# Squares of every second tile on GpSimd, another order on VectorE, shorter layer norms and null keys in a decoder block

## The chip, the cores and the metric

The kernel runs on one core of a Trainium2 chip. The metric is the device time of one launch in microseconds: 911.29 us, the median of three runs of the kernel before (907.23 to 911.75). Everything is float32; the large projections are made in three passes of a reduced type that together keep float32's accuracy.

The core has five engines with a queue each, and what stands in a queue is done in order: TensorE (PE; matmuls and transposes, results in PSUM), VectorE (DVE), ScalarE (ACT), GpSimd (POOL; it reaches SBUF alone, not PSUM) and SyncE (SP; here it issues all DMAs). They wait for one another by semaphores.

## The reference

16 batch elements of 256 tokens of 128 features go through one decoder block with a layer norm behind each of its three parts:

```
x = layernorm(x + attn(x));  x = layernorm(x + xattn(x, ctx));  x = layernorm(x + ffn(x))

attn:  xn = (x - mu) * rsqrt(var + 1e-5) * gamma
       q, k, v = xn @ w_q, xn @ w_kv            # 16 heads of 64
       k, v = [null_k, k], [null_v, v]          # 2 null keys and values per head
       q, k = l2norm(q) * q_scale, l2norm(k) * k_scale
       sim = 8 * q k^T - slope_h * distance;  causal mask;  softmax;  @ v;  @ w_out
xattn: 16 heads of 8 over 64 context tokens
ffn:   y = (x W1^T + b1) W2^T + b2              # no nonlinearity; one of 8 weight sets per 2 elements
```

The L2 norms need the sum of the squares of each head of q and k: per batch element 256 tokens (two tiles of 128) times 2048 values. The squares, their sums, a floor of 1e-24 and an inverse square root are separate steps.

## The kernel before

The work is written as one queue per engine, with an `iteration(i)` in each. There are 16 iterations. Iteration i does the attention of element i, the cross attention of element i-1, the end of the cross attention and the feed-forward of element i-2, and, ahead of time, the projections of q and k of element i+2 and of the values of element i+1, and the transposes of q and k of element i+1. The order inside each queue is written out by hand; there is no planner. A tile is 128 tokens; t is 0 or 1.

What the change touches, engine by engine:

- Layer norms (`ln_begin`, `newton`, `ln_end` on VectorE, `ln_seed` on ScalarE). VectorE makes mean and variance (L869, L872) and adds epsilon in an operation of its own (L875). ScalarE makes a first inverse square root by a logarithm and an exponential (`rsqrt_seed`, L1270 and L1272). VectorE refines it by one Newton step (three operations: L879, L881, L883) and normalises the tiles (L892). There are four norms: ln1 on the input, ln2 behind the attention, ln3 behind the cross attention, ln4 behind the feed-forward. The norms of q and k use the same seed and Newton step (`qk_seed`, `norms`).
- Squares of q and k. ScalarE copies the projections out of PSUM (`copy_qk`, L1308, eight chunks per element, four per tile) and squares them (`square_qk`, L1316, one operation per tile and half, 128x1024 each). VectorE sums them per head (`sum_squares`, L986) and applies the floor (`floor_squares`, L992). All go through one buffer `sq`. GpSimd scales q and k by the norms (`norm_qk`, L1569). For tile 1 the squares stand at the very end of ScalarE's iteration, two iterations ahead, in front of `copy_nullraw` (L1325), which empties the bank psJ0 that `project_v(i+1, 0)` of the next iteration (L443 to L445) takes.
- Masks. TensorE makes scores into three banks psS (`scores`, L555); VectorE adds the position bias and takes the row minimum (`mask_scores`, L1030, one operation per head); a bank is free again when its chunk is masked. Tile 0 has four chunks of four heads, tile 1 eight of two. ScalarE exponentiates head by head (L1350) and in between copies values (`copy_v`, L1330) and other results out of PSUM. VectorE makes the denominators (L1043 to L1047), GpSimd scales the probabilities (`norm_probs`, L1578), TensorE turns them (`turn_probs`, L577), and so on.
- Layer norm 3 in an iteration: `add_y2` (L1102) and `ln3_begin` come first on VectorE, `ln3_end` between the second and third chunk of tile 0. TensorE turns the result (`x2_turn`, L696) behind the first pair of scores of tile 1, ScalarE copies it (L1405), and the feed-forward (L704) uses it.
- GpSimd begins an iteration with `x1_plus_bias` (L1611), which waits for `add_y2`, then `x2_plus_bias` (L1618), which waits for `ln3_end`, then `norm_probs`.
- The start. The null keys are normalised, turned, and multiplied by the query weights of their head: 16 matmuls over 64 rows each, into two banks (`merged_nulls`, L460; each is two instructions). VectorE splits the product into two parts (`split_wn`). The null values are multiplied by the output weights (`null_values`, L468) right behind, into the bank psT0, and copied out by VectorE (`copy_null_v`). Both stand in TensorE's queue before the second half of the q and k projections of element 1.

Of the kernel before, what the change touches and what calls it, by code (L numbers as in the profile page):

```python
# [113 lines left out]
def program(nc, x, ctxT, gamma, w_q, w_kv, wqT, wvT, wout, nk, nvT, q_scale, k_scale,  # L114
            xwq, xwk, xwv, xbq, xbk, xbv, xwoT, xbo, w1b, w2T, b2, ident_in, dist_in, nullbias_in,
            hmask_in, hmask2_in, out):
    with ExitStack() as ctx:  # L117
# [99 lines left out]
        ln_small = sb("ln_small", [P, 5 * len(LN), NT])  # L217
        ve, lv, sd, nw, rs = ({n: ln_small[:, len(LN) * q + k, :] for k, n in enumerate(LN)} for q in range(5))
# [5 lines left out]
        nvT_s = pr[0][:, 8:10, :].rearrange("p h k -> p (h k)").rearrange("p (c n) -> p c n", c=HP)  # L224
# [51 lines left out]
        nkssq_ready = sem("nkssq_ready")  # L276
        nkrow_ready = sem("nkrow_ready")
# [52 lines left out]
        qk_normed = sem("qk_normed")  # L330
        probs_normed = sem("probs_normed")
# [99 lines left out]
        def _(pe):  # L431
# [16 lines left out]
            def turn_null_keys():  # L448

                pe.wait_ge(nkrow_ready, 1)  # L450
                take('T0', nkT_copied, 1)
# [268 lines left out]
            null_values()  # L720
# [12 lines left out]
            def iteration(i, w, g):  # L733
# [22 lines left out]
                if a:  # L756
                    project_v(i + 1, 3)
                turn_probs(i, 0)
# [96 lines left out]
        def _(dve):  # L855
# [10 lines left out]
            def ln_begin(name, src, tiles, count):  # L866
# [18 lines left out]
            def ln_end(name, src, dst, tiles, count):  # L885

                dve.wait_ge(seed_ready[name], count)
                a, z = tiles[0], tiles[-1] + 1
                steps.mark(newton(sd[name][:, a:z], ve[name][:, a:z], nw[name][:, a:z], rs[name][:, a:z], 0.5))
# [29 lines left out]

            def null_squares():  # L920
# [19 lines left out]
            def split_wn():  # L940
                dve.wait_ge(wn_ready, 1)
                hi, lo = (w[:].rearrange("p (c r n) -> p c r n", r=2, n=NULLS) for w in (wn_hi, wn_lo))
                ps = [psT[r][:, 0:NN // 2].rearrange("p (c n) -> p c n", n=NULLS) for r in range(2)]
                for r in range(2):
                    steps.mark(dve.tensor_copy(hi[:, :, r, :], ps[r]))
                steps.wait(dve)
                for r in range(2):
                    last = dve.tensor_tensor(lo[:, :, r, :], ps[r], hi[:, :, r, :].bitcast(F32), ALU.subtract)
                    if r == 0:
                        steps.mark(last)  # L950
                last.then_inc(wn_split, 1)
# [32 lines left out]
            def sum_squares(n, t, half):  # L984
                dve.wait_ge(qk_squared, 2 * (NT * n + t) + half + 1)
# [138 lines left out]

            ln1_begin(0)
# [6 lines left out]
            ln1_begin(1)  # L1132
            null_squares()
# [15 lines left out]
            copy_null_v()  # L1149
# [17 lines left out]
            def iteration(i, w, g):  # L1167
# [96 lines left out]
        def _(act):  # L1264
# [9 lines left out]
            def ln_seed(name, tiles, count):  # L1274
                act.wait_ge(var_ready[name], count)
                a, z = tiles[0], tiles[-1] + 1
                rsqrt_seed(ve[name][:, a:z], lv[name][:, a:z], sd[name][:, a:z], 1.0).then_inc(seed_ready[name], 1)
# [11 lines left out]
            def copy_nkT():  # L1289
                act.wait_ge(nkT_ready, 1)  # L1290
                act.activation(nkT[:], psT[0][:, 0:NN], ACT.Copy).then_inc(nkT_copied, 1)
# [18 lines left out]
            def square_qk(n, t, half):  # L1310
                act.wait_ge(qk_copied_act, chunks_to(QK_ACT, n, 4 * t + 2 * half + 1))
                act.wait_ge(qk_copied_dve, chunks_to(QK_DVE, n, 4 * t + 2 * half + 1))
                if half == 0:
                    need(act, ssq_ready, NT * n + t)
# [409 lines left out]
```

## Time and profile before

| | |
|---|---|
| runs | 907.23, 911.29, 911.75 us |
| profiled execution | 912.71 us, its span 910.9 us |
| TensorE (PE) | 801.6 us busy, 88% |
| VectorE (DVE) | 719.1 us, 79% |
| ScalarE (ACT) | 662.7 us, 73% |
| GpSimd (POOL) | 424.3 us, 47% |

The span runs from the first to the last instruction of the profiled execution. Busy is the time in which an engine worked; the shares are averages over a start of some 54 us, 16 iterations of 51 to 53 us and an end of some 40 us. A line such as L1316 is a line of the kernel; PEld is the loading of weights into TensorE, which overlaps with its matmuls.

### The profile page before, as it was taken

Reading aid. Unit: us, or ns where it says so; the run is one execution under the profiler, and the core shown is the slowest. Engines: PE = TensorE matmul, PEld = TensorE weight load, DVE = VectorE, ACT = ScalarE, POOL = GpSimd, SP = SyncE. Lnnn points to the kernel's source line nnn. Section 1 sums busy time; section 2 is a strip of 40 time slices with the busy share of each in tenths; the row PEclk is TensorE's granted clock in tenths of the full one; section 3 lists DMA queues with packets and bytes.
Section 4 is the critical chain, followed back from the end, with each engine's and each line's share of the span. In section 5 each row is a group of like instructions: output and inputs, shape, how many; then the busy total and the mean of one; then the engine's idle time right before and its main releaser. Section 6 shows DMA issues by size and latency. Waiting matters only on the chain. (4 is left out here: it accounts for less than half of the span.)

```text
span 910.9 us, 19543 instructions
## 1 busy us (share of the span) xinstructions
PE 801.6 (88%) x6469; PEld 581.0 (64%) x6469; DVE 719.1 (79%) x2504; ACT 662.7 (73%) x1994; POOL 424.3 (47%) x356
## 2 busy tenths in 40 slices
PE   5879989898998989898998989899998989887953
PEld 3657657575776757576675757576675757665632
DVE  6584677898969897898969897888969887887744
ACT  4386686968777786968778796978778696867522
POOL 0317164472727355371736446271736547173611
PEclk9599999999999999999999999999999999999965
DMA  6000001000100001000100000000010001000000
GB/s 211 6 7 1 13 2 36 2 7 13 31 13 8 13 8 36 2 6 13 31 13 8 13 7 24 13 7 14 10 34 7 8 1 31 7 6 8 7 1 12
DMA packets 26418, 15.62 MB, mean 17 GB/s; under 512 B 4304, under 2 KB 25552, under 8 KB 26320
## 3 DMA queue, kind: packets, MB, share of 16 engines
q1 hardware_dynamic: 26320, 14.38, 5.5%
q8 instruction: 53, 0.87, 0.4%
q14 instruction: 45, 0.37, 0.1%
HBM read 12.27 MB, written 2.10 MB: 16 GB/s over the span
## 5 line engine op out<-in xcount | busy, mean ns | idle before, releaser
L1578 POOL TENSOR_TENSOR pr<-pr,rden 128x512 f32<-128x512 f32 x192 | 192.9, 1040 | 170.3 <-DVE rden L1045 170.3
L1350 ACT ACTIVATE pr<-pr,nmin 128x256 f32<-128x256 f32 (+1 forms) x512 | 225.3, 446 | 0.0
L1030 DVE CUSTOM_DVE_ANT_0 pr<-psS,alibi,nullmin 128x256 f32<-128x256 f32 (+1 forms) x512 | 180.3, 412 | 17.0 <-PE psS L555 16.9
L577 PE MATMUL psT<-ident,pr 128*128 128x128 f32 x768 | 124.6, 287 | 19.9 <-POOL pr L1578 19.7
L555 PE MATMUL psS<-kT,qT 64*128 64x256 f32 (+1 forms) x1024 | 110.6, 344 | 32.1 <-DVE nmin L1030 30.4
L1569 POOL TENSOR_TENSOR qk<-qk,rn 128x1024 f32<-128x1024 f32 x64 | 121.0, 1911 | 32.9 <-DVE rn L883 32.9
L577 PEld LDWEIGHTS psT<-ident,pr 128*128 128x128 f32 x768 | 80.9, 141 | 57.9 <-POOL pr L1578 28.6
L555 PEld LDWEIGHTS psS<-kT,qT 64*128 64x128 f32 x1024 | 78.3, 187 | 58.6 <-issue 56.6
L1308 ACT ACTIVATE qk<-psJ 128x512 f32<-128x512 f32 x128 | 75.5, 591 | 40.3 <-PE psJ L445 40.1
L1350 ACT ACTIVATION_READ_ACCUMULATOR pr<-pr,nmin 128x1 f32 x512 | 98.7, 193 | 0.0
L986 DVE TENSOR_REDUCE ssq<-sq 128x16 f32<-128x1024 f32 x64 | 77.6, 1212 | 22.8 <-ACT sq L1316 22.8
L1380 ACT ACTIVATE xp<-xp 128x1024 f32<-128x1024 f32 x32 | 33.8, 1058 | 73.1 <-DVE xp L1090 73.1
L1611 POOL TENSOR_TENSOR x1b<-x,bo 128x256 f32<-128x256 f32 x16 | 11.7, 732 | 159.8 <-DVE r L1102 147.2
L600 PE MATMUL psY<-pT,val 128*64 128x128 f32 x1024 | 82.0, 286 | 4.2 <-ACT aoT L1336 2.5
L1585 POOL TENSOR_TENSOR xp<-xp,xrden 128x1024 f32<-128x1024 f32 x32 | 60.9, 1903 | 42.0 <-DVE xrden L1097 42.0
L600 PEld LDWEIGHTS psY<-pT,val 128*64 128x64 f32 x1024 | 53.5, 136 | 37.7 <-issue 26.7
L537 PE MATMUL psS<-ident,qk 128*128 128x128 f32 x512 | 69.8, 276 | 3.5 <-DVE qT L1020 2.9
L1367 ACT ACTIVATE pT<-psT 128x512 f32<-128x512 f32 x112 | 65.5, 585 | 6.5 <-PE psT L577 6.5
L443 PE MATMUL psJ<-wqk_hi,xnT_hi 128*128 128x512 f32 x128 | 63.9, 499 | 5.2 <-DVE xnT_lo L980 2.9
L1316 ACT ACTIVATE sq<-qk 128x1024 f32<-128x1024 f32 x64 | 65.8, 1052 | 0.4
L537 PEld LDWEIGHTS psS<-ident,qk 128*128 128x128 f32 x512 | 56.7, 140 | 9.4 <-DVE qT L1020 4.0
L1270 ACT ACTIVATE ln_small<-ln_small 128x2 f32<-128x2 f32 x64 | 12.7, 199 | 68.3 <-DVE ln_small L875 68.2
(147 smaller groups left out, 1692.7 us busy)
## 6 DMA issues: line engine op xcount, KB each, us to landing
w1s<-w1b SPq DMA_DIRECT2D x8, 258.0 KB, 3.0
xres<-x SPq DMA_DIRECT2D x16, 128.0 KB, 2.1
w2s<-w2T SPq DMA_DIRECT2D x8, 256.0 KB, 3.2
out<-x SPq DMA_DIRECT2D x16, 128.0 KB, 1.8
xin<-x SPq DMA_DIRECT2D x15, 128.0 KB, 2.4
pr<-w_kv SPq DMA_DIRECT2D x2, 512.0 KB, 5.8
pr<-w_q SPq DMA_DIRECT2D x1, 512.0 KB, 3.6
wo<-wout SPq DMA_DIRECT2D x1, 512.0 KB, 6.4
```

What stands on the lines that cost most here:

```text
L537: mm = pe.transpose(psS[isk][:, P * j:P * (j + 1)], qk[n % 2][t][:, col:col + P], ident[:])
L555: mm = pe.matmul(psS[score_bank(t, c)][:, keys * j:keys * (j + 1)], qT[r, h // 2, P * t:P * (t + 1)], kT[r, h // 2, 0:keys], start=True, s ...
L577: mm = pe.transpose(psT[c % 2][:, P * j:P * (j + 1)], pr[t][:, h, P * kt:P * (kt + 1)], ident[:])
L600: mm = pe.matmul(bank[r, P * pair:P * (pair + 1)], val[b % 2][:, kt, DH * h:DH * (h + 1)], pT[c % 4][:, P * j:P * (j + 1)], start=(kt == 0 ...
L986: steps.mark(dve.tensor_reduce(ssq[:, t, H * half:H * (half + 1)], sq[:, HD * half:HD * (half + 1)].rearrange("p (h d) -> p h d", d=DH), A ...
L1030: dve.tensor_tensor_reduce(pr[t][:, h, :], psS[score_bank(t, c)][:, keys * j:keys * (j + 1)], alibi[:, h, SEQ - keys:SEQ], 1.0, nullmin[:, ...
L1308: act.activation(qk[n % 2][t][:, 512 * j:512 * (j + 1)], psJ[c % 2][:], ACT.Copy).then_inc(qk_copied_act, 1)
L1316: act.activation(sq[:, col], qk[n % 2][t][:, col], ACT.Square).then_inc(qk_squared, 1)
L1350: act.activation(pr[t][:, h, :], pr[t][:, h, :], ACT.Exp, bias=nmin[:, t, h:h + 1], scale=-1.0, accum_out=dparts[:, t, h, 0:1]).then_inc(e ...
L1367: act.activation(pT[c % 4][:], psT[c % 2][:], ACT.Copy).then_inc(pT_copied_act, 1)
L1569: pool.tensor_tensor(v, v, rn[:, t, H * k:H * (k + 1)].unsqueeze(2).broadcast_to([P, H, DH]), ALU.mult).then_inc(qk_normed, 1)
L1578: pool.tensor_tensor(pr[t][:, hs, :], pr[t][:, hs, :], rden[:, t, hs].unsqueeze(2).broadcast_to([P, heads, P * (t + 1)]), ALU.mult).then_i ...
```

## The change

- ScalarE squares tile 0 alone. GpSimd squares tile 1 with a multiplication, for element 0 at the start and for element i+1 at the beginning of iteration i, behind `x1_plus_bias`; from iteration 2 on it first waits for the variances of layer norm 3. The new semaphore `qk_squared_pool` tells VectorE.
- On VectorE, all four chunks of tile 0 are masked and shifted before `ln3_end`; the first sum of squares of tile 1 comes behind the second chunk of tile 1, the second behind the third; the floor behind all masks of the iteration. `copy_pT(i, 0)` comes before `add_h2`. ScalarE's `qk_seed(i+1, 1)` comes behind its exponentials.
- Epsilon is no longer added by VectorE: ScalarE's logarithm takes it as a bias (from a small tile `eps`), and the Newton step adds it in its second operation. `ln_seed` waits for both variances and for `eps`.
- The null keys are laid out in a cleared tile so that one matmul over 128 rows makes two heads: 8 matmuls into one bank. The copy that lays them out becomes two. `split_wn` has two operations instead of four.
- `null_values` moves into iteration 0, ahead of its first `turn_probs`, and `copy_null_v` behind the fourth chunk of tile 1 there. Its input moves to another part of SBUF.

```diff
             def ln_begin(name, src, tiles, count):
                 for t in tiles:
-                    steps.mark(dve.bn_aggr(mv[name][:, t, :], st[name][:, t, :]))
-                steps.wait(dve)
-                a, z = tiles[0], tiles[-1] + 1
-                dve.tensor_scalar(ve[name][:, a:z], mv[name][:, a:z, 1], EPS, None, ALU.add).then_inc(var_ready[name], 1)
+                    dve.bn_aggr(mv[name][:, t, :], st[name][:, t, :]).then_inc(var_ready[name], 1)
...
-            def newton(y0, v, tmp, res, half):
-                steps.mark(dve.tensor_tensor(tmp, y0, y0, ALU.mult))
+            def newton(y0, v, tmp, res, half, floor=None):
+                steps.mark(dve.scalar_tensor_tensor(out=tmp, in0=y0, scalar=-half, in1=y0, op0=ALU.mult, op1=ALU.mult))
                 steps.wait(dve)
-                steps.mark(dve.scalar_tensor_tensor(out=tmp, in0=tmp, scalar=-half, in1=v, op0=ALU.mult, op1=ALU.mult))
+                if floor is None:
+                    steps.mark(dve.tensor_tensor(tmp, v, tmp, ALU.mult))
+                else:
+                    steps.mark(dve.scalar_tensor_tensor(out=tmp, in0=v, scalar=floor, in1=tmp, op0=ALU.add, op1=ALU.mult))
...
             def merged_nulls():
                 pe.wait_ge(h_loaded, 16 * 2)
                 take('T0', wn_split, 1)
-                take('T1', wn_split, 1)
-                for h in list(range(0, H, 2)) + list(range(1, H, 2)):
-                    r = slice(DH * (h % 2), DH * (h % 2) + DH)
-                    mm = pe.matmul(psT[h % 2][:, NULLS * (h // 2):NULLS * (h // 2 + 1)], wqT_s[r, h // 2, :],
-                                   nkT[r, NULLS * h:NULLS * (h + 1)], start=True, stop=True)
+                for c in range(HP):
+                    pair = slice(2 * NULLS * c, 2 * NULLS * (c + 1))
+                    mm = pe.matmul(psT[0][:, pair], wqT_s[:, c, :], nkT[:, pair], start=True, stop=True)
                 mm.then_inc(wn_ready, 1)
...
             merged_nulls()
-            null_values()
             project_nulls(0)
...
                 if a:
                     project_v(i + 1, 3)
+                if i == 0:
+                    null_values()
                 turn_probs(i, 0)
...
# VectorE's iteration
-                mask_scores(i, 0, (0, 1))
+                mask_scores(i, 0, (0, 1, 2, 3))
+                null_shift(i, 0)
                 if e:
                     ln3_end(i - 2)
-                mask_scores(i, 0, (2, 3))
-                null_shift(i, 0)
-                if p:
-                    sum_squares(i + 1, 1, 0)
                 need(dve, probsT_ready, PC * i)
                 for k in range(8):
                     mask_scores(i, 1, (k,))
                     if k == 1:
                         if p:
-                            sum_squares(i + 1, 1, 1)
-                            floor_squares(1)
+                            sum_squares(i + 1, 1, 0)
                         denominators(i, 0)
+                    if k == 2 and p:
+                        sum_squares(i + 1, 1, 1)
                     if k == 3:
+                        if i == 0:
+                            copy_null_v()
+                        copy_pT(i, 0)
                         if e:
                             add_h2(i - 2)
-                        copy_pT(i, 0)
                     if k == 5:
                         copy_pT(i, 2)
                 null_shift(i, 1)
+                if p:
+                    floor_squares(1)
...
# ScalarE
-            def rsqrt_seed(v, tmp, res, scale):
-                steps.mark(act.activation(tmp, v, ACT.Ln, scale=scale))
+            def rsqrt_seed(v, tmp, res, scale, floor=0.0):
+                steps.mark(act.activation(tmp, v, ACT.Ln, bias=floor, scale=scale))
...
                 if a:
                     copy_v(i + 1, 3)
-                if p:
-                    qk_seed(i + 1, 1)
                 copy_pnT(i, 0)
...
                 copy_aoT(i, 0, 1)
+                if p:
+                    qk_seed(i + 1, 1)
...
                     copy_qk(i + 2, 7)
-                    square_qk(i + 2, 1, 0)
-                    square_qk(i + 2, 1, 1)
                     copy_nullraw(i + 2)
...
# GpSimd
+            def square_qk(n, half):
+                pool.wait_ge(qk_copied_act, chunks_to(QK_ACT, n, 4 + 2 * half + 1))
+                if half == 0:
+                    pool.wait_ge(ssq_ready, NT * n + 1)
+                v = qk[n % 2][1][:, HD * half:HD * (half + 1)]
+                pool.tensor_tensor(sq[:, HD * half:HD * (half + 1)], v, v, ALU.mult).then_inc(qk_squared_pool, 1)
...
+            square_qk(0, 0)
+            square_qk(0, 1)
             norm_qk(0, 0)
             norm_qk(0, 1)
...
                 if c:
                     x1_plus_bias(i - 1)
+                if p:
+                    if e:
+                        pool.wait_ge(var_ready["ln3"], NT * (i - 1))
+                    square_qk(i + 1, 0)
+                    square_qk(i + 1, 1)
                 if e:
                     x2_plus_bias(i - 2, (i - 2) // 2)
                 norm_probs(i, 0)
```

## Rows read from the trace of the kernel before

**Rows 1.** Page, 40 slices of the span: TensorE's granted clock in tenths.

```profile
PEclk9599999999999999999999999999999999999965
```

**Rows 2.** Waits, whole span: who <- whom, us in total, times, longest.

```profile
PE psS L555 <- DVE nmin L1030: 30.4, 32, 1.5
```

**Rows 3.** Timeline, TensorE, iteration 7: start, us, instruction, [idle before <- releaser].

```profile
420.26 0.44 PE L627 MATMUL psT<-ident,x 128*128 128x128 f32 x2
420.75 0.50 PE L443 MATMUL psJ<-wv_hi,xnT_hi 128*128 128x512 f32 x1
...
425.09 1.14 PE L555 MATMUL psS<-kT,qT 64*128 64x256 f32 x8 [0.78 <-DVE nmin L1030]
426.16 0.44 PE L696 MATMUL psT<-ident,x 128*128 128x128 f32 x2
426.35 0.49 PE L443 MATMUL psJ<-wv_hi,xnT_hi 128*128 128x512 f32 x1
...
431.98 0.66 PE L577 MATMUL psT<-ident,pr 128*128 128x128 f32 x4 [1.17 <-POOL pr L1578]
...
434.77 0.27 PE L616 MATMUL psJ<-ident,pnn 128*32 128x128 f32 x1 [0.48 <-ACT val L1330]
```

**Rows 4.** Timeline, ScalarE, the same iteration.

```profile
418.59 1.99 ACT L1316 ACTIVATE sq<-qk 128x1024 f32<-128x1024 f32 x2
...
421.75 0.60 ACT L1330 ACTIVATE val<-psJ 128x512 f32<-128x512 f32 x1 [0.45 <-PE psJ L445]
422.25 0.39 ACT L1350 ACTIVATE pr<-pr,nmin 128x128 f32<-128x128 f32 x1
...
427.70 0.37 ACT L1405 ACTIVATE x1T<-psT 128x256 f32<-128x256 f32 x1
...
429.50 0.23 ACT L1355 ACTIVATE dparts<-nulld 128x32 f32<-128x32 f32 x1
...
434.03 0.59 ACT L1330 ACTIVATE val<-psJ 128x512 f32<-128x512 f32 x1
```

**Rows 5.** Timeline, TensorE, iteration 1.

```profile
109.13 0.44 PE L627 MATMUL psT<-ident,x 128*128 128x128 f32 x2
109.95 0.50 PE L443 MATMUL psJ<-wv_hi,xnT_hi 128*128 128x512 f32 x1 [0.38 <-ACT nullraw L1325]
...
123.71 0.27 PE L616 MATMUL psJ<-ident,pnn 128*32 128x128 f32 x1 [0.97 <-ACT val L1330]
```

**Rows 6.** Page, groups of instructions: count | busy us, mean ns | idle before, releaser.

```profile
L986 DVE TENSOR_REDUCE ssq<-sq 128x16 f32<-128x1024 f32 x64 | 77.6, 1212 | 22.8 <-ACT sq L1316 22.8
...
L1585 POOL TENSOR_TENSOR xp<-xp,xrden 128x1024 f32<-128x1024 f32 x32 | 60.9, 1903 | 42.0 <-DVE xrden L1097 42.0
```

**Rows 7.** Timeline, GpSimd, iteration 7.

```profile
419.27 0.73 POOL L1611 TENSOR_TENSOR x1b<-x,bo 128x256 f32<-128x256 f32 x1 [9.29 <-DVE r L1102]
```

**Rows 8.** Timeline, VectorE, iteration 7.

```profile
420.50 0.35 DVE L1030 CUSTOM_DVE_ANT_0 pr<-psS,alibi,nullmin 128x128 f32<-128x128 f32 x1 [0.30 <-PE psS L555]
...
422.68 0.16 DVE L879 TENSOR_TENSOR ln_small<-ln_small 128x2 f32<-128x2 f32 x1
...
423.78 0.34 DVE L1030 CUSTOM_DVE_ANT_0 pr<-psS,alibi,nullmin 128x128 f32<-128x128 f32 x1
...
430.26 0.20 DVE L1043 TENSOR_REDUCE den<-dparts 128x16 f32<-128x48 f32 x1
...
430.90 0.48 DVE L1030 CUSTOM_DVE_ANT_0 pr<-psS,alibi,nullmin 128x256 f32<-128x256 f32 x1
```

**Rows 9.** Chain that ended last, near the span's end: start, us, what.

```profile
901.11 0.18 DVE ln_small L875
```

**Rows 10.** Timeline, TensorE, the start.

```profile
28.88 6.16 PE L460 MATMUL psT<-nkT,pr 64*128 64x2 f32 x32
...
35.77 3.59 PE L468 MATMUL psT<-wo,pr 128*32 128x128 f32 x16 [0.73 <-DVE wn_lo L948]
```

**Rows 11.** One line, L958 on VectorE: ns min/median/max, first and last start.

```profile
L958 DVE TENSOR_TENSOR wv_lo<-pr,wv_hi x2: 693/1483/2273, 25.6 to 29.9; 128x512 fp32r<-128x512 f32 x2
```

More of the change, by code:

```diff
@@ L216, in program @@
         mv = {n: sb(f"{n}_mv", [P, NT, 2]) for n in LN}
-        ln_small = sb("ln_small", [P, 5 * len(LN), NT])
-        ve, lv, sd, nw, rs = ({n: ln_small[:, len(LN) * q + k, :] for k, n in enumerate(LN)} for q in range(5))
+        eps = sb("eps", [P, 1])
+        ln_small = sb("ln_small", [P, 4 * len(LN), NT])
+        lv, sd, nw, rs = ({n: ln_small[:, len(LN) * q + k, :] for k, n in enumerate(LN)} for q in range(4))
         wqk_raw = pr[1][:, 0:8, :].rearrange("p h k -> p (h k)")
@@ L223, in program @@
         wqT_s = pr[0][:, 0:8, :]
-        nvT_s = pr[0][:, 8:10, :].rearrange("p h k -> p (h k)").rearrange("p (c n) -> p c n", c=HP)
+        nvT_s = xp[1][:, 8:12, :].rearrange("p h k -> p (h k)").rearrange("p (c n) -> p c n", c=HP)
         dist = x3[:].rearrange("p t d -> p (t d)")
@@ L276, in program @@
         nkssq_ready = sem("nkssq_ready")
+        eps_ready = sem("eps_ready")
+        nkT_cleared = sem("nkT_cleared")
         nkrow_ready = sem("nkrow_ready")
@@ L330, in program @@
         qk_normed = sem("qk_normed")
+        qk_squared_pool = sem("qk_squared_pool")
         probs_normed = sem("probs_normed")
@@ L450, in turn_null_keys @@
                 pe.wait_ge(nkrow_ready, 1)
-                take('T0', nkT_copied, 1)
+                take('T0', nkT_copied, 2)
                 pe.transpose(psT[0][:, 0:NN], nkrow, ident[0:NN, 0:NN]).then_inc(nkT_ready, 1)
@@ L887, in ln_end @@
                 dve.wait_ge(seed_ready[name], count)
+                dve.wait_ge(var_ready[name], NT * count)
                 a, z = tiles[0], tiles[-1] + 1
-                steps.mark(newton(sd[name][:, a:z], ve[name][:, a:z], nw[name][:, a:z], rs[name][:, a:z], 0.5))
+                steps.mark(newton(sd[name][:, a:z], mv[name][:, a:z, 1], nw[name][:, a:z], rs[name][:, a:z], 0.5, EPS))
                 steps.wait(dve)
@@ L918, in split_wqk, with clear_nkT @@
                                   ALU.subtract).then_inc(wsplit_ready, 1)
+            def clear_nkT():
+                dve.memset(nkT[:], 0.0).then_inc(nkT_cleared, 1)
             def null_squares():
@@ L941, in split_wn @@
                 dve.wait_ge(wn_ready, 1)
[L942 to L945, printed above, removed]
+                steps.mark(dve.tensor_copy(wn_hi[:], psT[0][:, 0:NN]))
                 steps.wait(dve)
[L947 to L951, printed above, removed]
+                dve.tensor_tensor(wn_lo[:], psT[0][:, 0:NN], wn_hi[:].bitcast(F32), ALU.subtract).then_inc(wn_split, 1)
             def split_wv(c):
@@ L984, in sum_squares @@
             def sum_squares(n, t, half):
-                dve.wait_ge(qk_squared, 2 * (NT * n + t) + half + 1)
+                dve.wait_ge(qk_squared if t == 0 else qk_squared_pool, 2 * n + half + 1)
                 steps.mark(dve.tensor_reduce(ssq[:, t, H * half:H * (half + 1)],
@@ L1122, in ln4_end @@
                 ln_end("ln4", r3, x3, (0, 1), b + 1).then_inc(x3_ready, 1)
+            dve.memset(eps[:], EPS).then_inc(eps_ready, 1)
             ln1_begin(0)
@@ L1132, in _ @@
             ln1_begin(1)
+            clear_nkT()
             null_squares()
@@ L1274, in ln_seed @@
             def ln_seed(name, tiles, count):
-                act.wait_ge(var_ready[name], count)
+                act.wait_ge(eps_ready, 1)
+                act.wait_ge(var_ready[name], NT * count)
                 a, z = tiles[0], tiles[-1] + 1
-                rsqrt_seed(ve[name][:, a:z], lv[name][:, a:z], sd[name][:, a:z], 1.0).then_inc(seed_ready[name], 1)
+                rsqrt_seed(mv[name][:, a:z, 1], lv[name][:, a:z], sd[name][:, a:z], 1.0, eps[:]).then_inc(seed_ready[name], 1)
             def null_keys_seed():
@@ L1290, in copy_nkT @@
                 act.wait_ge(nkT_ready, 1)
-                act.activation(nkT[:], psT[0][:, 0:NN], ACT.Copy).then_inc(nkT_copied, 1)
+                act.wait_ge(nkT_cleared, 1)
+                for r in range(2):
+                    rows = slice(DH * r, DH * (r + 1))
+                    act.activation(nkT[rows, :].rearrange("p (c r n) -> p c r n", r=2, n=NULLS)[:, :, r, :],
+                                   psT[0][rows, 0:NN].rearrange("p (c r n) -> p c r n", r=2, n=NULLS)[:, :, r, :],
+                                   ACT.Copy).then_inc(nkT_copied, 1)
             def context_kv():
@@ L1308, in copy_qk @@
                 act.activation(qk[n % 2][t][:, 512 * j:512 * (j + 1)], psJ[c % 2][:], ACT.Copy).then_inc(qk_copied_act, 1)
-            def square_qk(n, t, half):
-                act.wait_ge(qk_copied_act, chunks_to(QK_ACT, n, 4 * t + 2 * half + 1))
-                act.wait_ge(qk_copied_dve, chunks_to(QK_DVE, n, 4 * t + 2 * half + 1))
+            def square_qk(n, half):
+                act.wait_ge(qk_copied_act, chunks_to(QK_ACT, n, 2 * half + 1))
                 if half == 0:
-                    need(act, ssq_ready, NT * n + t)
+                    need(act, ssq_ready, NT * n)
                 col = slice(HD * half, HD * (half + 1))
-                act.activation(sq[:, col], qk[n % 2][t][:, col], ACT.Square).then_inc(qk_squared, 1)
+                act.activation(sq[:, col], qk[n % 2][0][:, col], ACT.Square).then_inc(qk_squared, 1)
             def qk_seed(n, t):
@@ L1431, in _ @@
             copy_qk(1, 5)
-            square_qk(1, 0, 0)
+            square_qk(1, 0)
             copy_qk(1, 6)
             copy_qk(1, 7)
-            square_qk(1, 0, 1)
+            square_qk(1, 1)
             copy_v(0, 0)
@@ L1506, in iteration @@
                     copy_qk(i + 2, 2)
-                    square_qk(i + 2, 0, 0)
+                    square_qk(i + 2, 0)
                 copy_aoT(i, 1, 0)
@@ L1515, in iteration @@
                     copy_qk(i + 2, 3)
-                    square_qk(i + 2, 0, 1)
+                    square_qk(i + 2, 1)
                 copy_pT(i, 11)
@@ L1619, in x2_plus_bias @@
                                    ALU.add).then_inc(x2b_ready, 1)
+            square_qk(0, 0)
+            square_qk(0, 1)
             norm_qk(0, 0)
```

8 lines of the change are left out of this document (1 added, 7 removed).

## The prediction

> **What bounds the kernel now.** I read four views in this order: the busy shares and the clock of the page, the waits of the whole span, the timeline of one iteration engine by engine, and the first and last stretches. The clock row [rows 1] shows full clock from the start's end to the epilogue, so between them a microsecond of TensorE work has one price. TensorE is 88% busy. The waits [rows 2] name what stops it most: the masks on VectorE, twice in each of 16 iterations, 30.4 us in all.
>
> The timeline of iteration 7, which starts at 419.2 and repeats from iteration 2 to 14 within 0.03 us, puts this in place. Behind 438.8 TensorE shows no idle time until the next iteration's first scores. All its idle time lies in a front of about 20 us: 0.78 us and once more about a microsecond for masks, 1.17 us for the probabilities that GpSimd scales, 0.48 us for a value copy on ScalarE [rows 3]. So only what shortens the front shortens an iteration, and the last gate in it counts. That gate is the row at 434.77: the turn of the null probabilities waits for `copy_v(i+1, 3)`, which starts on ScalarE at 434.03 [rows 4]. From the first exponential at 422.25 to that copy ScalarE shows no idle time: 16 exponentials of tile 0, three copies, the null exponentials at 429.50, eight exponentials of tile 1, another copy. It is a solid chain of 11.8 us, and its start is set by `copy_v(i+1, 0)` at 421.75, which had waited for `project_v(i+1, 0)` on TensorE.
>
> Iteration 1 is a natural test. It has no end of layer norm 3 among its masks, so VectorE is ahead there; yet TensorE only waits longer for the same copy, 0.97 us in place of 0.48 [rows 5]. What VectorE gives in the front is not passed on; what ScalarE gives is.
>
> **The change, part by part.**
>
> *Squares of tile 1.* Two of the four squares per batch element leave ScalarE: 1.99 us at the end of an iteration, 418.59 to 420.58 [rows 4]. Behind them stands the copy of the raw null scores, and only that frees the bank of `project_v(i+1, 0)`. TensorE starts the turn of x1 at 420.26 and the projection at 420.75, 0.49 us later; the same pair of a turn and a projection, ungated, takes 426.35 - 426.16 = 0.19 us [rows 3]. Without the squares the null scores are copied about a microsecond earlier, so the projection comes 0.30 us earlier, and with it the chain, the null exponentials (429.20), the value copy (433.73) and the turn of the nulls. The rest of the 1.99 us becomes idle time of ScalarE in front of `copy_v`. In iteration 1 the distance is 109.95 - 109.13 = 0.82 us [rows 5], which gives 0.63.
>
> *The same squares on GpSimd.* The trace has no square there. The nearest row is a two-input operation of the same size, 1.90 us [rows 6]; from below, ScalarE's 1.0 us for one; from above, twice the row, since both operands are full streams here and one is a broadcast there. I take 1.90. GpSimd is free after `x1_plus_bias`, at 419.27 + 0.73 = 420.00 [rows 7], and has nothing due until layer norm 3 ends, so the squares run from 420.0 to 423.8, beside the masks, and nothing waits for them until the third chunk of tile 1.
>
> The Trainium skill (GPSIMD Engine Reference, section 3.1, Elementwise) puts a two-input operation at about 2.6 cycles an element. For 1024 elements that is an estimate of 2.2 us, where the rows here have 1.90; the squares would end at 424.4, and the sum stays.
>
> *Order on VectorE.* The first eight masks take 422.68 - 420.50 = 2.18 us, the end of layer norm 3 after them 423.78 - 422.68 = 1.10 us [rows 8]. Now all 16 masks come first (to 424.9), the null shift, then the end of layer norm 3 from 425.07 to 426.2. The third chunk is masked 1.1 us earlier, and the 0.78 us wait at 425.09 goes. But the next thing in TensorE's queue is the turn of x2, which starts at 426.16 now and at about 426.3 then: one wait takes the other's place. Behind it the second pair of scores of tile 1 comes about 0.9 us earlier, since the first sum of squares (1.21 us [rows 6]) no longer stands before the first chunk. The denominators find VectorE free as soon as the null exponentials end, and start at 429.5 where they now start at 430.26; turning the probabilities starts at 431.2 in place of 431.98 [rows 3, 8]. TensorE then reaches the turn of the nulls at 433.4 and waits there a microsecond, for a copy that is 0.30 us earlier and no more. The second sum of squares now stands before the third head group: from 429.5, 0.64 us for the denominators (430.26 to 430.90 [rows 8]), 0.8 for a chunk, 1.2 for the sum and 0.5 for the first mask end at 432.6, and ScalarE wants it at 432.75. That margin is thin. The floor and the square-root seed of tile 1 move behind the masks and into idle time of ScalarE before the cross exponentials: nothing.
>
> *No constant step in layer norms.* One operation of 0.17 us and its hand-over, 0.20 us, leaves each of four norms per iteration; in the body all lie beside TensorE work. At the end three follow each other with nothing beside them (the norm of the last iteration's attention and the last two, as at 901.11 [rows 9]): 0.6 us, less a second wait per seed on ScalarE, which no row shows (0 to 0.05 us). I take 0.5 there, and 0.03 per iteration off the gain above, where the seed of layer norm 4 stands in the chain.
>
> *The start.* The product of the null keys shrinks from 32 to 16 instructions (6.16 us, about 3 saved), the null values leave (3.59 us) [rows 10]. The first saving is not collected: VectorE is late in its place. A split of the value weights that met a GpSimd operation took 2.27 us and 0.69 without [rows 11]; now the squares of element 0 run at 24 us, meet the Newton steps, and push the same splits back, so the split null keys come about 0.2 us later than now. The second saving is collected, but at 46 us the squares of element 1 meet the end of layer norm 1 on VectorE, a whole GpSimd operation (1.9), and in iteration 0 the null values share a bank with the turn of the probabilities, which waits until VectorE copies them out behind three chunks and a sum of squares: about 0.8 more. 3.6 - 0.2 - 1.9 - 0.8 = 0.7 us gained. Ends: 3.5 gained (no meeting) and 2 lost (iteration 0 alone).
>
> The Trainium skill (SBUF — State Buffer, Who interferes with whom) says VectorE and GpSimd lock one pair of ports for a whole instruction, and that a VectorE operation with one SBUF input outside a two-port mode is free of it. The 2.27 us above agree. Were there no lock, the start would gain 3 us and the sum be about 7.7; by the rule, 5.3.
>
> **Sum.** 13 iterations of 0.27 are 3.5, iteration 1 gives 0.6, the start 0.7, the end 0.5: 5.3 us. The profiled execution took 912.71 us (span 910.9, 1.8 around it), 1.4 over the median of 911.29; 5.3 less is 907.4 for it and 906.0 for a median.
>
> **Rivals.**
>
> *Nothing arrives.* The projection's 0.3 us may not be there (ends of matmuls are modelled), or the thin margin at the third head group eats it: a mask 0.3 us late stops ScalarE, and the chain ends where it ends now. For it: the margin of 0.15 us. Against: iteration 1, where a later projection went with a later chain. What is left is start and end, 0 to 3 us: 909.5.
>
> *The front pays in full.* If the turn of the nulls isn't the last gate, the 0.8 us at turning the probabilities are kept: 13 x 0.8 + 1.2 = 11.6, so 899.7. Against it stands iteration 1 [rows 5].
>
> *Slower: the squares outlast the masks.* The null shift and the end of layer norm 3 start at 425.0, with both inputs in SBUF, the kind that waits for GpSimd. From 420.0 that allows 2.5 us a square; from there each excess delays x2. ScalarE takes the copy of x2 at 427.70 [rows 4], now 427.4, in the middle of its chain, with 0.65 us in hand. At twice the row (3.8 us) the squares end at 427.6, x2 is turned by 429.25, ScalarE stops for 1.85 us, less 0.3 gained: 13 x 1.55 = 20, so 931. For it: no row has two full streams on GpSimd. Against: every row of 1024 elements, with other broadcasts, is 1.9.
>
> **How the numbers follow.** Forecast 0.52 (903 to 909.5), nothing arrives 0.21, full front 0.12, slower 0.15. A run of this kernel tells about 0.5%, 4.6 us, from no change. The forecast, 5.3 with 2 on either side, is over that in six of ten: 0.33; with the full front, 0.45 or a little more. Same: the rest of the forecast and nothing arrives, 0.40. Slower: 0.14. The range runs from the full front to a slower case of small excess, 899.5 to 914.
>
> **What would show it.** Right: the projection 0.2 us behind the turn of x1 in every iteration; a wait of the turn of x2 for layer norm 3 that is new, about 0.9 us; the wait for the third chunk gone; the wait of the turn of the nulls grown to a microsecond; an iteration 0.27 us shorter; squares of 1.9 us on GpSimd ending before the null shift. Wrong: squares over 2.5 us, an idle gap of ScalarE inside its chain, or iterations shortened by 0.5 us or more, which would mean that I have the wrong gate.

## The result and the profile after

The changed kernel takes 912.62 us, the median of 20 runs from 910.76 to 913.64; the kernel before 909.22, the median of 20 from 907.23 to 913.15. The ratio is 1.003, with a 95% interval of 1.0017 to 1.0043: a loss of about 3 us where a gain of 5.3 was forecast. The profiled execution of the changed kernel took 911.29 us (span 909.5).

The medians can only be read with TensorE's granted clock: the later runs of the kernel before, which list it, lie mostly in two groups, 907.3 to 910.3 us with a mean granted clock of 0.972 and 911.4 to 913.5 with 0.966 (a few with 0.968 lie at 910.3 to 912.2), the profile ahead of the prediction (912.71 us, 0.966) is of the second, and the changed kernel's 20 runs all lie between 0.959 and 0.963.

The body did what was forecast. TensorE's first scores of iterations 7 and 8 start at 419.46 and 471.7, and the two lengths that alternate from iteration 2 on are 50.80 and 52.22 us where they were 51.07 and 52.49 (one or two early ones are 0.2 to 0.4 longer in both): 0.27 less each. First the waits of TensorE in the whole span of the changed kernel: who waited for whom, us in total, times, longest; then its timeline in iteration 7.

```profile
PE psT L698 <- DVE x L896: 19.9, 15, 3.3
PE psT L579 <- POOL pr L1589: 17.1, 16, 2.3
PE psJ L618 <- ACT val L1339: 13.8, 14, 1.1
PE psS L557 <- DVE nmin L1030: 9.1, 19, 1.1
```

```profile
420.55 0.44 PE L629 MATMUL psT<-ident,x 128*128 128x128 f32 x2
420.74 0.48 PE L447 MATMUL psJ<-wv_hi,xnT_hi 128*128 128x512 f32 x1
...
422.11 1.16 PE L557 MATMUL psS<-kT,qT 64*128 64x128 f32 x16 [0.42 <-DVE nmin L1030]
...
424.70 1.13 PE L557 MATMUL psS<-kT,qT 64*128 64x256 f32 x8
427.02 0.44 PE L698 MATMUL psT<-ident,x 128*128 128x128 f32 x2 [1.18 <-DVE x L896]
...
431.46 0.66 PE L579 MATMUL psT<-ident,pr 128*128 128x128 f32 x4 [0.90 <-POOL pr L1589]
...
434.74 0.27 PE L618 MATMUL psJ<-ident,pnn 128*32 128x128 f32 x1 [0.97 <-ACT val L1339]
```

Against [rows 2, 3] the reader sees each mark that the prediction asked for. The projection stands 0.19 us behind the turn of x1 (it was 0.49), the 0.78 us wait for the masks of the third chunk, ahead of tile 1's first scores, is gone, the turn of x2 has a new one of 1.18 (0.9 forecast), and the turn of the null probabilities waits 0.97. One wait was not forecast: at 422.11 TensorE stands 0.42 us before the second pair of chunks of tile 0, since the masks that free their banks stand at the same distance behind the first scores as before (2.65 us) and do not come earlier with the projection. The masks' waits fell from 30.4 us to 9.1, but 19.9 came at the turn of x2 in their place.

So the loss lies ahead of iteration 2, whose first scores start at 162.2 where they started at 160.6. The first scores of iterations 0 and 2, of the kernel before and then of the changed one:

```profile
54.71 1.16 PE L555 MATMUL psS<-kT,qT 64*128 64x128 f32 x16 [0.29 <-ACT kT L1341]
...
160.59 1.16 PE L555 MATMUL psS<-kT,qT 64*128 64x128 f32 x16
```

```profile
52.58 1.77 PE L557 MATMUL psS<-kT,qT 64*128 64x128 f32 x16 [0.29 <-ACT kT L1350]
...
162.17 1.16 PE L557 MATMUL psS<-kT,qT 64*128 64x128 f32 x16
```

The next rows are GpSimd, VectorE and TensorE of the changed kernel at the end of iteration 0, where nothing in the prediction looked.

```profile
104.28 0.73 POOL L1622 TENSOR_TENSOR x1b<-x,bo 128x256 f32<-128x256 f32 x1 [12.60 <-DVE x L896]
104.97 3.78 POOL L1581 TENSOR_TENSOR sq<-qk 128x1024 f32<-128x1024 f32 x2
```

```profile
104.45 0.61 DVE L879 SCALAR_TENSOR_TENSOR newt<-seedq 128x32 f32<-128x32 f32 x1 [0.25 <-ACT seedq L1275]
105.09 1.82 DVE L882 TENSOR_TENSOR newt<-ssq,newt 128x32 f32<-128x32 f32 x1
106.94 1.85 DVE L886 SCALAR_TENSOR_TENSOR rn<-newt,seedq 128x32 f32<-128x32 f32 x1
108.72 0.68 DVE L1020 COPY qT<-psS 128x512 f32<-128x512 f32 x1
```

```profile
109.65 1.16 PE L557 MATMUL psS<-kT,qT 64*128 64x128 f32 x16 [2.68 <-DVE qT L1020]
```

The squares of element 2 start as soon as `x1_plus_bias` ends. VectorE is then in `norms(2, 0)`: two of its operations, which take 0.19 us each when no GpSimd operation runs beside them, take 1.82 and 1.85 and end with GpSimd's. The last copy of qT is queued behind them, and TensorE waits 2.68 us for it. From iteration 2 on GpSimd first waits for the statistics of layer norm 3, so this pair doesn't meet. The same Newton step of the other tile does meet a GpSimd operation (L1605) in the body, 0.97 us at 450.01 in iteration 7, but there TensorE has other work and shows no wait.

The Trainium skill (SBUF — State Buffer, Who interferes with whom) says that a VectorE instruction with both inputs in SBUF contends with a GpSimd instruction that reads SBUF, that the one issued first keeps the ports for its whole length, and that a reduction never contends. The trace agrees: the held operations end with a GpSimd instruction, and a sum of squares beside GpSimd's scaling, at 30.33, took its 1.21 us.

The waits have a second price. Stretches of the changed kernel, in columns us, TensorE's busy time, granted clock, DMA share and GB/s:

```profile
48.60:50.60 2.00, 0.00 (x1) 1.00 0.00 0
53.00:56.40 3.40, 3.40 (x21) 0.51 0.01 2
106.90:109.60 2.70, 0.07 (x1) 1.00 0.01 3
111.00:114.40 3.40, 3.40 (x21) 0.50 0.00 0
```

Twice TensorE stood idle at full clock and then worked at half clock, 1.2 GHz, a few microseconds later; that the idle time brings the half clock is not shown by these rows, but the first experiment takes one of the two waits away, and its stretch goes with it. The stretch at 53.0 lies on the first scores of iteration 0, the one at 111.0 on the front of iteration 1. The idle time ahead of the first is the meeting that was priced (GpSimd's squares of element 1 hold L884), and between the two stands the bank of the null values:

```profile
47.35 1.77 DVE L884 SCALAR_TENSOR_TENSOR ln_small<-ln_mv,ln_small 128x2 f32<-128x2 f32 x1
...
66.74 0.27 DVE L963 COPY null_v<-psT 32x128 f32<-32x128 f32 x1
```

```profile
50.62 1.09 PE L539 MATMUL psS<-ident,qk 128*128 128x128 f32 x8 [2.01 <-DVE qT L1020]
...
62.96 1.94 PE L470 MATMUL psT<-wo,xp 128*32 128x128 f32 x16
67.16 0.63 PE L579 MATMUL psT<-ident,pr 128*128 128x128 f32 x4 [2.27 <-POOL pr L1589]
```

The last row names GpSimd, but it had scaled the first chunk by 65.0 (63.98 and a microsecond); what ends at 67.0 is the copy of the null values out of the same bank.

### The profile page after: what moved, and what is told of

The parts are those of the page before. It is cut to its first block and busy times, and to the rows that moved or that the text cites. A ratio compares the mean times of both kernels' runs of the same rounds, so it can differ in the third digit from the quotient of the medians.

```text
span 909.5 us, 19500 instructions
## 1 busy us (share of the span) xinstructions
PE 795.4 (87%) x6453; PEld 579.0 (64%) x6453; DVE 716.8 (79%) x2440; ACT 644.2 (71%) x1963; POOL 484.5 (53%) x388
## 5 line engine op out<-in xcount | busy, mean ns | idle before, releaser
L1581 POOL TENSOR_TENSOR sq<-qk 128x1024 f32<-128x1024 f32 x32 | 60.0, 1895 | 30.0 <-DVE ssq L992 29.1
L1273 ACT ACTIVATE ln_small<-ln_mv,eps 128x2 f32<-128x2 f32 x64 | 18.7, 292 | 65.4 <-DVE ln_mv L875 65.4
```

## The experiments

All times are medians, beside runs of the kernel before on the same chip; ratios are to that kernel, with 95% intervals. Periods are from first scores to first scores.

### Hold the squares of element 2

```
                 if p:
+                    if i >= 1:
+                        pool.wait_ge(rn_ready, NT * (i + 1) + 1)
                     if e:
```

> From iteration 1 on, GpSimd's squares of batch element i+1 wait until VectorE has normalised element i+1's first tile (in the changed kernel they met that Newton step once, at 104.97 us). Theory (the squares hold VectorE, VectorE holds the last copy of qT, and TensorE waits 2.68 us at 109.65 and falls to half clock behind it): iteration 0 is shorter by 2.7 us (57.07 to 54.4), iteration 1 by 0.6 more where the half-clock stretch at 111 is gone, all others stay: about 3.3 us less than the changed kernel, 909.3. Rival (the Newton step isn't what is late; the wait moves to another gate): the wait at the first scores of iteration 1 stays above 2 us, time within 0.7 us of the changed kernel.

909.74 us, ratio 0.9993 (0.9974 to 1.0012). Iteration 0 took 54.64 us and iteration 1 51.87. GpSimd, then TensorE:

```profile
106.36 3.75 POOL L1581 TENSOR_TENSOR sq<-qk 128x1024 f32<-128x1024 f32 x2 [0.58 <-DVE rn L886]
```

```profile
107.67 1.16 PE L557 MATMUL psS<-kT,qT 64*128 64x128 f32 x16
```

And the Newton step on VectorE that had taken 1.82:

```profile
105.86 0.19 DVE L882 TENSOR_TENSOR newt<-ssq,newt 128x32 f32<-128x32 f32 x1
```

The wait and the half-clock stretch behind it are gone: iteration 0 is 2.43 us shorter, iteration 1 0.65, and the median is 2.9 lower. The theory holds. The wait of 2.01 us ahead of iteration 0's first scores is still there, and the half-clock stretch behind it is 6.9 us long in this profile (50.6 to 57.5) where it was 3.4.

### The null values on the other bank

```
-                take('T0', nullv_copied, 1)
+                take('T1', nullv_copied, 1)
-                    mm = pe.matmul(psT[0][0:NN, 0:P], ...
+                    mm = pe.matmul(psT[1][0:NN, 0:P], ...
-                dve.tensor_copy(null_v[:], psT[0][0:NN, 0:P]) ...
+                dve.tensor_copy(null_v[:], psT[1][0:NN, 0:P]) ...
```

> The null values keep their new place in iteration 0 but go to the other of the two turning banks. Theory (the first turn of the probabilities waits for VectorE's copy of the null values, though the page names GpSimd, which had scaled the first chunk at about 65.0): the turn starts at about 65.2 in place of 67.16, iteration 0 is 1.9 us shorter and the time is 910.7. Rival (GpSimd's scaling, as the page names it): the wait of 2.27 us stays and the time is within 0.5 us of the changed kernel.

911.47 us, ratio 1.0008 (0.9989 to 1.0027); iteration 0 took 56.33. TensorE:

```profile
65.16 0.66 PE L579 MATMUL psT<-ident,pr 128*128 128x128 f32 x4 [0.37 <-POOL pr L1589]
...
67.25 0.63 PE L579 MATMUL psT<-ident,pr 128*128 128x128 f32 x4 [0.37 <-DVE null_v L963]
```

The turn starts where it was expected, so the releaser on the page was the wrong one. Of its 2 us only 0.74 reach the end of iteration 0, where 1.9 was expected: the second turn now waits for that copy, and the null turn behind it for a value copy.

### Epsilon on VectorE again

```
+                dve.tensor_scalar(ve[name][:, a:z], mv[name][:, a:z, 1], EPS, None, ALU.add).then_inc(var_ready[name], NT)
...
-                rsqrt_seed(mv[name][:, a:z, 1], lv[name][:, a:z], sd[name][:, a:z], 1.0, eps[:])
+                rsqrt_seed(ve[name][:, a:z], lv[name][:, a:z], sd[name][:, a:z], 1.0)
```

> Layer norms alone as before: VectorE adds epsilon with an operation of its own, ScalarE's logarithm has no column for its bias; all else as in the changed kernel. Theory (the logarithm with a column takes 0.29 us in place of 0.20 and eats half of the 0.17 us operation): the last two norms take 0.05 us longer each, iterations stay within 0.05 us, the time within 0.5 us of the changed kernel. Rival 1 (my prediction, 0.2 us per norm at the end): 0.6 us slower. Rival 2 (the column costs more than it saves, over the whole body): 1 us or more faster.

933.69 us, ratio 1.0259 (1.0230 to 1.0289), most periods 52.01 and 53.42. None of the three expectations is near. GpSimd, VectorE and TensorE in iteration 7:

```profile
443.88 3.76 POOL L1575 TENSOR_TENSOR qk<-qk,rn 128x1024 f32<-128x1024 f32 x2
```

```profile
444.65 1.16 DVE L878 TENSOR_SCALAR ln_small<-ln_mv 128x2 f32<-128x2 f32 x1
445.72 0.47 DVE L1033 CUSTOM_DVE_ANT_0 pr<-psS,alibi,nullmin 128x256 f32<-128x256 f32 x1
```

```profile
446.75 1.13 PE L557 MATMUL psS<-kT,qT 64*128 64x256 f32 x8 [1.04 <-DVE nmin L1033]
```

An addition of 0.17 us, met by GpSimd's first scaling (443.88 to 445.8), takes 1.16; the masks queued behind it are late, and TensorE waits 1.04 us for them. This operation has one input in SBUF; the same section of the Trainium skill lists its kind among those that can take both port pairs, and so wait for GpSimd, and the row agrees.

### Epsilon on VectorE in layer norms 1 to 3

```
+                if name != "ln4":
+                    dve.tensor_scalar(ve[name][:, a:z], mv[name][:, a:z, 1], EPS, None, ALU.add) ...
```

> VectorE adds epsilon with an operation of its own in layer norms 1, 2 and 3, and not in layer norm 4; all else as in the changed kernel. With all four norms so, an iteration took 1.21 us more (52.01 for 50.80) and the time was 933.7. Theory (only the operation of layer norm 4 matters: in the new order of VectorE it starts at 444.65 while GpSimd scales queries, is held for 1.16 us, and the masks of the last chunk behind it are late): periods go back to 50.8 and 52.2 within 0.1 us, time within 1 us of 912.6. Rival (the operations of the other norms delay the chain of ScalarE too): periods stay over 51.5, time over 922.

917.77 us, ratio 1.0079 (1.0052 to 1.0105), periods 50.97 and 52.40. Of the 1.21 us, 1.04 go with layer norm 4 alone, as the theory had it; the other three cost 0.18 more per iteration and not under 0.1, and the time missed the expected 912.6 by 5 us. In its profile the start is longer too (iterations 0 and 1 are 57.61 and 53.79): its two half-clock stretches there are twice as long as in the changed kernel's (51.7 to 58.6 and 109.8 to 116.6), and there is one more at 840.2 to 847.0. Why they are longer was not followed.

### All squares on ScalarE, the rest as changed

```
+                    square_second(i + 2, 0)
+                    square_second(i + 2, 1)
                     copy_nullraw(i + 2)
```

The added function is ScalarE's square of the second tile; it is also called for elements 0 and 1 in the start (not shown), and the calls in GpSimd's part go.

> All squares on ScalarE as before; the order on VectorE, the layer norms and the null keys and values as in the changed kernel. Theory (the 0.27 us per iteration come from ScalarE's freed end alone, VectorE's order is not passed on): periods of iterations 2 to 14 return to 51.07 and 52.49 within 0.06 us; no operation of VectorE is held in the start, so the waits of TensorE at 50.62 (2.01 us) and 109.65 (2.68 us) go and the first scores start 1.5 to 2 us earlier than 52.6. Sum against the changed kernel: 3.5 + 0.6 more, 2.7 + 1.7 + 1.2 less: 911.3. Rival (VectorE's order gives the 0.27 us): periods stay at 50.80 and 52.22, time 907.5.

911.71 us, ratio 1.0015 (0.9996 to 1.0034), most periods 51.12 and 52.53: without the squares' move the rest of the change gives the body nothing (before: 51.07 and 52.49). First scores of iteration 0:

```profile
48.57 1.16 PE L557 MATMUL psS<-kT,qT 64*128 64x128 f32 x16 [0.29 <-ACT kT L1357]
```

One Newton step of the start, in the changed kernel and here:

```profile
25.73 1.82 DVE L882 TENSOR_TENSOR newt<-ssq,newt 128x32 f32<-128x32 f32 x1
```

```profile
24.50 0.19 DVE L882 TENSOR_TENSOR newt<-ssq,newt 128x32 f32<-128x32 f32 x1
```

The first scores are 4.0 us earlier than in the changed kernel, where 1.5 to 2 was expected. Two meetings make it up: in the changed kernel the squares of element 0 hold the Newton steps at 24 us, and the null projections start at 34.90 where they start at 32.51 here (2.4), and the wait at 50.62 is 2.01 us long where 0.40 are left here (1.6). The wait of 2.68 us ahead of iteration 1 is gone.

### The kernel before with the squares alone

```
+                if c and p:
+                    pool.wait_ge(rn_ready, NT * (i + 1) + 1)
+                    if e:
+                        pool.wait_ge(var_ready["ln3"], i - 1)
+                    square_qk(i + 1, 0)
+                    square_qk(i + 1, 1)
```

ScalarE's two squares at the end of the iteration go (not shown).

> The kernel before with one part of the change: the second tile's squares of elements 2 and up on GpSimd, behind VectorE's normalisation of the first tile and behind the statistics of layer norm 3; VectorE's order, epsilon, null keys and values as before. Theory (the 0.27 us come from ScalarE's freed end, but only the new order takes the end of layer norm 3 out of the squares' way): the end of layer norm 3 at 422.7 in iteration 7 is held until the squares end at about 423.8, the masks behind it come a microsecond later, and periods grow to 51.3 to 52.1 in place of 51.07, time 913 to 923. Rival (the squares alone give the gain): periods 50.80 and 52.22, time 906.

922.76 us, ratio 1.0130 (1.0104 to 1.0155), periods 52.19 and 53.60, a little over the expected range. VectorE, then TensorE in iteration 7, then a stretch of iteration 8:

```profile
423.66 1.42 DVE L880 TENSOR_TENSOR ln_small<-ln_small 128x2 f32<-128x2 f32 x1
```

```profile
427.34 1.13 PE L556 MATMUL psS<-kT,qT 64*128 64x256 f32 x8 [2.05 <-DVE nmin L1031]
```

```profile
481.70:484.90 3.20, 3.20 (x13) 0.50 0.02 5
```

The end of layer norm 3 is held until the squares end at 425.07 (GpSimd runs them from 421.32 for 3.75 us), and the scores behind the masks of the third chunk wait 2.05 us (0.78 before). The same wait stands in all iterations from 2 to 14; half clock follows it in iteration 8 and six others, and not in the remaining six. So ScalarE's freed end alone loses and, by the experiment before, VectorE's order alone gains nothing: the 0.27 us need both.

### The value copy first

```
-                exponentials(i, 1, (3,))
                 if a:
                     copy_v(i + 1, 3)
+                exponentials(i, 1, (3,))
```

> The copy of the value projection's last quarter on ScalarE goes ahead of the two exponentials that stand before it; all else as in the changed kernel. Theory (ScalarE's solid chain, 422 to 441 us in iteration 7, is the gate as a whole, and the wait of the null turn is only where it shows): the 0.97 us wait for the value copy goes, the waits behind it (0.28 us for the copy of the head outputs at 438.71) grow by as much, periods stay 50.80 and 52.22 within 0.15 us. Rival (the value copy is the last gate by itself, as my prediction had it): an iteration is 0.5 to 0.97 us shorter, the time 898 to 905.

911.02 us, ratio 1.0003 (0.9984 to 1.0021), most periods 50.57 and 52.00: 0.22 less, between the two. TensorE in iteration 7, where the null turn starts at 433.50 with no wait:

```profile
433.99 0.66 PE L602 MATMUL psY<-pT,val 128*64 128x128 f32 x8 [0.22 <-DVE r L1115]
...
435.73 1.13 PE L557 MATMUL psS<-kT,qT 64*128 64x256 f32 x8 [0.49 <-DVE nmin L1030]
```

The copy was the last gate, but with 0.22 us on the next: then VectorE comes last, which shows no idle time there between 426.6 and 438.7, and not ScalarE's chain as my theory said.

### The kernel before, once more

> The kernel before, unchanged. Its runs show two groups, 907.3 to 908.2 us at a mean granted clock of 0.972 and 911.4 to 913.5 at 0.966; the profile shown is of the second. Theory (the two groups are the same work with other half-clock stretches): in a profile of the first group the waits and periods of the iterations are the same within 0.1 us, and half-clock stretches of about 10 us in all are missing, which is worth the 5 us. Rival (another cause, such as late transfers at the start): the stretches are the same and a wait differs.

This profile is of the first group by its clock (0.972), at 910.03 us with a span of 908.2. Its waits, before the masks for one, are those of [rows 3, 5] within 0.02 us, and its periods from iteration 1 on within 0.05. Three stretches of it, by columns as above:

```profile
20.00:31.00 11.00, 7.79 (x44) 0.84 0.24 65
31.20:41.30 10.10, 8.33 (x30) 0.50 0.01 2
67.80:71.20 3.40, 3.29 (x32) 1.00 0.02 7
```

The earlier profile has 0.50 all through the first two, and half clock at 67.8 to 71.2. In all it has 63.5 us at half clock against 53.1 here. First scores start at 51.6 against 54.7, and iteration 0 is 52.58 long against 53.33. The theory holds in its kind, with 10.4 us of half clock less, but that is worth 2.7 us of span between these two profiles and not 5; why one execution starts with more full clock than another stays open.

### The start repaired

```
-                if p:
+                if c and p:
+                    pool.wait_ge(rn_ready, NT * (i + 1) + 1)
...
             qk_seed(0, 0)
+            square_second(0, 0)
...
-            square_qk(0, 0)
-            square_qk(0, 1)
             norm_qk(0, 0)
```

With it goes the other bank of the second experiment.

> Three repairs of the changed kernel's start, its body left alone: the second tile's squares of batch elements 0 and 1 stay on ScalarE (GpSimd takes over from element 2), GpSimd's squares wait for VectorE's normalisation of the same element's first tile, and the null values go to the other turning bank. Theory (what the change gains in the body is lost in the start, by squares that meet VectorE's Newton steps and by a bank): first scores at 48.6 us as with all squares on ScalarE, iteration 0 of 53 to 54 us, iteration 1 of 51.9, periods of 50.80 and 52.22 after that: some 8 us under the changed kernel, 904.5, and under the kernel before. Rival (TensorE's half-clock stretches only move, and take back what the start saves): no more than 4 us under the changed kernel, 908.5 or above.

902.82 us, ratio 0.9919 (0.9897 to 0.9942), 1.7 below the expected time. First scores at 49.1, iterations 0 and 1 of 52.89 and 51.85, periods 50.79 and 52.22. Between the start and the epilogue the clock stays full:

```profile
41.00:863.00 822.00, 749.88 (x6303) 1.00 0.05 13
```

With the value copy first as well:

> The three repairs of the start and the value copy ahead of two exponentials, in one kernel. Each alone: the repairs gave 902.8, the copy took 0.22 us off 13 iterations (50.57 and 52.00). Theory (they lie in different stretches and add): periods of 50.57 and 52.00, first scores at 49 us, time 902.8 - 2.9 = 900. Rival (they share a gate): periods stay at 50.79 and 52.21, time 902.5 to 903.

900.27 us, ratio 0.9872 (0.9846 to 0.9898), periods 50.59 and 52.01: the two add, and this version beats both kernels.

## Why the prediction was wrong

The step that failed is the start, "3.6 - 0.2 - 1.9 - 0.8 = 0.7 us gained", with the 0.6 of iteration 1 behind it. Between the two profiles shown, first scores come 2.1 us earlier, iteration 0 is 3.7 longer (57.07 for 53.33) and iteration 1 equal (52.52 for 52.55): 1.6 lost at iteration 2 in place of 1.3 gained, a miss of 2.9. One term that the sum put at nothing is as large as that; a second thing, the clock, hides in the medians.

- *A meeting that was not listed.* I read GpSimd's free time in iteration 7, where the squares stand behind layer norm 3, and carried it to all iterations. In iteration 1 that wait does not exist, and the squares meet `norms(2, 0)`: 2.68 us of wait, and half clock behind it. Without it (first experiment) iterations 0 and 1 were 2.43 and 0.65 us shorter, 3.1 together, and iteration 2 started 2.6 us earlier (159.54); iteration 1 then has the 0.6 that was forecast.
- *The clock.* The prediction gave a wait in the start its own length and nothing more; the half-clock stretches that followed were not in the sum. And the base was off: 911.29 stood for a kernel whose median over 20 runs is 909.22, because nearly half of its listed executions have the higher mean clock of 0.972, which the one whose profile was read did not have, and none of the changed kernel's 20 has. Against the second profile of the kernel before, the changed one is 5.4 us late at iteration 2 (162.17 for 156.76). By the medians the start costs some 7 (3.4 lost, although body and end give 4); the profiles show 1.6 to 5.4 of that, and the rest lies in executions that were not profiled. So with the meeting held the kernel was level with the one before (ratio 0.9993), not 5.3 us ahead.

The listed terms were near. The meeting at 47 us took 1.77 for 1.9. The bank of the null values was put at 0.8: the turn of the probabilities starts 14.58 us behind the first scores in place of 12.32, but on the other bank only 0.74 of that reached the end of iteration 0. The meeting at 24 us came as listed: the split null keys, forecast 0.2 us later than before, came 0.8 earlier (34.85 for 35.63), though beside squares on ScalarE the meeting costs 2.4. All these meetings could have been avoided: in the kernel with the start repaired iteration 2 starts at 153.88, 6.7 us earlier than in the profile that was read. Two of the three repairs were run alone as well; the third, the squares of elements 0 and 1 on ScalarE, was not, so its share is open. The prediction's own figures for a start without meetings, 3.5 and 3, do not follow from its terms, which give 3.6 - 0.8 = 2.8.

The rest stands. Squares took 1.895 us on GpSimd (1.90) and ended at 424.12, before the null shift at 425.68. The body gave 0.27 per iteration, and the gate was the value copy. The end gave 0.58, read against the second profile of the kernel before, which has the same half clock there (81.85 for 82.43 us from iteration 15's first scores): the 0.5 came in another way. Ahead of the norms 0.23 was lost (61.18 for 60.95 us from those scores to L1115). Each of the last two norms gave only 0.05 to 0.07, since the logarithm with a column is slower than the 0.20 us one; 0.71 came from an addition that GpSimd had held, and with it a copy on ScalarE. One line of each kernel, the logarithm after and the held addition before (second profile):

```profile
L1273 ACT ACTIVATE ln_small<-ln_mv,eps x64: 277/295/306, 3.8 to 905.5; 128x2 f32<-128x2 f32 x64
```

```profile
888.02 0.82 DVE L875 TENSOR_SCALAR ln_small<-ln_mv 128x2 f32<-128x2 f32 x1
```

"0.03 per iteration" for the constant step was right only as the kernel stands: in the new order the same step would have cost 1.21, of which 1.04 in layer norm 4. And "what ScalarE gives is" passed on did not hold by itself: with VectorE's old order an iteration grew by 1.12. The edits of the body were priced one by one, and each has its worth only beside the others.

Of the rivals, none had the right place. That the squares outlast the masks did not happen; the slower case that did was the same lock at another step.

## What to carry to other kernels

Before work is moved to GpSimd, list what VectorE runs beside it in the start, in the first iterations and in the end, not only in a steady iteration: operations with two SBUF inputs above all, and here an addition with one was held too. A guard that the body happens to have is missing where its stage has not begun. Then put the moved work behind an event that stands after the last such step. A wait that is cut in the body is worth its length at most: 0.97 us cut at the null turn gave 0.22, as the next gate took the rest. One that is made in a place where TensorE has nothing else can cost its length and a stretch at half clock.

## What the runs showed that was not expected

- A VectorE operation of 0.17 us on 128x2 elements can cost an iteration 1.0 us, when it meets GpSimd ahead of masks that TensorE needs.
- Half clock follows waits in the middle of the kernel: 2.0 and 2.7 us of idle TensorE, each with a stretch at 1.2 GHz soon after, and 7 of 13 waits of 2.05 us with the squares alone. Between iterations 2 and 14 of the changed kernel, with waits of up to 1.2 us each, there is none.
- The same kernel runs mostly in two groups some 4 us apart, in the two profiles with the same waits and another clock in the start; three runs gave a median that was 2 us from that of twenty.
- ScalarE's logarithm of 128x2 elements takes 0.295 us with a column as its bias and 0.203 without.
